# Half rotations of the tile two ahead put in front of the division of the probabilities on GpSimd

## The reference, cut to what matters

```python
for i in range(DEPTH):                                   # DEPTH = 6, 16 heads of 64, window 32
    x = attn_layer(shift_tokens(x), Wqkv[i], q_scale[i], k_scale[i], Wo[i]) + x
    x = ffn_layer(shift_tokens(x), ln_g[i], ln_b[i], W1[i], b1[i], W2[i], b2[i]) + x

def attn_layer(x, Wqkv, qs, ksc, Wo):
    q, k, v = split(x @ Wqkv)
    q = l2norm(q) * qs
    k = l2norm(k) * ksc
    q = q * cos * scale + rotate_half(q) * sin * scale
    k = k * cos * inv + rotate_half(k) * sin * inv
    sim = einsum(q, keys of this and the last window) * 8.0   # masked
    attn = softmax(sim)
    return (attn @ v) @ Wo
```

## Time and profile before

| | us |
|---|---|
| median of 3 runs | 2736.19 |
| the profiled execution | 2730.72 |
| its span | 2728.9 |
| VectorE busy | 1973.4 (72%) |
| TensorE busy, matmuls | 2169.6 (80%) |
| GpSimd busy | 1492.2 (55%) |
| ScalarE busy | 1509.5 (55%) |

### The profile page before, as it was taken

How to read it: one execution, slowest core, us unless ns; L and a number is a source line. 1 busy time by engine, 2 the same in 40 slices (tenths; PEclk the granted TensorE clock), 3 DMA queues, 4 the chain that set the end, 5 groups by cost and what they waited for, 6 DMA issues and landing times.

```text
span 2728.9 us, 53797 instructions
## 1 busy us (share of the span) xinstructions
PE 2169.6 (80%) x21684; PEld 1154.6 (42%) x21780; DVE 1973.4 (72%) x2087; ACT 1509.5 (55%) x1863; POOL 1492.2 (55%) x1031
## 2 busy tenths in 40 slices
PE   4768875888998989888889889889988756678734
PEld 1111123555555555555555555555555411111334
DVE  1766628888888888888888888888889426676211
ACT  2255564566676666666766676666766321455600
POOL 5500017777776776777776777777777234100033
PEclk7787897999999999999999999999999866897967
DMA  4100000000001000100010000000000001000133
GB/s 149 60 19 25 13 2 1 17 2 17 2 2 26 17 2 2 26 2 17 1 26 2 17 2 9 19 17 2 1 9 2 1 18 67 22 27 13 32 92 86
DMA packets 55828, 59.08 MB, mean 22 GB/s; under 512 B 13142, under 2 KB 45012, under 8 KB 55508
## 3 DMA queue, kind: packets, MB, share of 16 engines
q1 hardware_dynamic: 53444, 50.77, 6.1%
q0 software_dynamic: 2128, 4.72, 0.7%
HBM read 44.07 MB, written 11.01 MB: 20 GB/s over the span
## 4 chain that ended last, share of the span: by engine, by line
PE 36%; POOL 19%; DVE 17%; issue 16%; ACT 9%; DMA 2%; SPq 1%; POOLq 0%; DVEq 0%; ACTq 0%
PE bank L735 5%; PE bank L706 4%; PE bank L859 4%; DVE big L1463 4%; PE bank L923 4%; PE bank L933 4%; POOL big L580 3%; POOL big L597 3%; POOL big L581 3%; DVE big L1569 3%; POOL small L590 2%; ACT big L1180 2%; ACT pxs L1305 2%; PE bank L976 2%; DVE small L1563 2%
## 5 line engine op out<-in xcount | busy, mean ns | idle before, releaser
L1463 DVE TENSOR_REDUCE big<-bank 128x1 f32<-128x512 f32 x512 | 327.7, 685 | 199.3 <-PE bank L706 195.3
L602 POOL TENSOR_TENSOR sc<-sc,small 128x1024 f32<-128x1024 f32 x96 | 263.4, 2744 | 365.4 <-DVE small L1605 365.4
L859 PE MATMUL bank<-wqk,xs 128*128 128x512 f32 x768 | 359.2, 610 | 13.6 <-ACT xs L1261 8.3
L933 PE MATMUL bank<-pxs,mw 128*128 128x256 f32 x1536 | 366.2, 382 | 0.0
L1296 ACT ACTIVATE sc<-sc 128x1024 f32<-128x1024 f32 x96 | 101.5, 1057 | 464.0 <-DVE sc L1595 463.9
L933 PEld LDWEIGHTS bank<-pxs,mw 128*128 128x128 f32 x1536 | 291.1, 192 | 102.7 <-issue 71.9
L1180 ACT ACTIVATE big<-bank 128x1024 f32<-128x1024 f32 x256 | 250.2, 1026 | 140.1 <-PE bank L720 137.1
L1569 DVE TENSOR_TENSOR big<-big,rotCl 128x2048 f32<-128x2048 f32 x96 | 226.2, 2356 | 78.1 <-POOL big L581 78.1
L706 PE MATMUL bank<-pxs 48*128 48x512 bf16 x512 | 183.6, 439 | 117.1 <-DVE big L1463 74.0
L1563 DVE TENSOR_REDUCE small<-big 128x32 f32<-128x2048 f32 x96 | 219.0, 2281 | 39.5 <-ACT big L1274 30.2
L1584 DVE TENSOR_TENSOR big<-big,small 128x1024 f32<-128x1024 f32 x192 | 246.5, 1284 | 1.1 <-POOL small L592 1.1
(11 more groups left out here) (244 smaller groups left out, 3945.1 us busy)
## 6 DMA issues: line engine op xcount, KB each, us to landing
wqk<-in_L_ffn_Wqkv SPq DMA_DIRECT2D x12, 512.0 KB, 4.4
pxs<-part_rows SPq DMA_DIRECT2D x64, 96.0 KB
pxs<-part_rows SPq DMA_DIRECT2D x64, 64.0 KB
wqk<-in_L_ffn_w SPq DMA_DIRECT2D x16, 256.0 KB, 3.0
wvt<-in_wv_layers_t SPq DMA_DIRECT2D x6, 512.0 KB, 4.7
wol<-in_L_ffn_Wo SPq DMA_DIRECT2D x6, 512.0 KB, 5.8
part_rows<-big SPq DMA_DIRECT2D x24, 128.0 KB
part_rows<-sc SPq DMA_DIRECT2D x24, 128.0 KB
```

Of the source, the lines that this page charges most:

```text
L602: pool.tensor_tensor(p3, p3, rden(i).unsqueeze(2).broadcast_to([P, LH, 64]), ALU.mult).then_inc(l_pn, 1)
L859: m = pe.matmul(bank[:, 2 - 2 * half + c, :], xs[:, b % 2, WIN + i * P:WIN + (i + 1) * P], wqk[:, (2 * half + c) * 512:(2 * half + c + 1) ...
L933: m = pe.matmul(bank[:, 6, part * 2 * P:(part + 1) * 2 * P], mw[:, 2 * (a % 4) + s, a // 4, :], pxs[:, part, a, s, :], start=(a == 0 and s ...
L1463: dve.tensor_reduce(nm[:, qt, 2 * p + r:2 * p + r + 1], bank[:, 4 + r, :], AX.X, ALU.max, negate=True).then_inc(a_mx, 1)
```

## The change

On GpSimd, `normalise(T, i)` moves from in front of `turn_swapped(T + 2, ...)` to behind it, within the same slot. Nothing is added or removed.

```diff
@@ -611,12 +611,12 @@
                 if ahead >= 1:
                     inverse_root(T + 1, (i + 1) % 2)
                     add_keys(T + 1, (i + 1) % 2)
-                normalise(T, i)
                 if ahead >= 2:
                     if b == BATCH - 1 and i == 2:
                         pool.wait_ge(l_tab, 3 * l + 6)
                         settle(pool)
                     turn_swapped(T + 2, (i + 2) % TILES)
+                normalise(T, i)
```

## The result

The changed kernel takes 2763.96 us, the median of seven runs (2755.71 to 2768.84), against 2736.19 for the kernel before (seven runs). The ratio is 1.0103, 95% interval 1.0077 to 1.0129: 1% slower, 28 us. The prediction said 2772, and 2742 to 2825. The profiled execution took 2762.28 us with a span of 2760.5, 31.6 more than the one of before; the stretch from the first E to the last (E is the end of L1595) grew from 1715.4 to 1749.9 us, by 34.5, so that all of it lies in the layers.

A forecast was written before the change was run, and what follows sets the result against it. The prediction took a ring through reciprocals, division, half rotations and L1569 as the bound. Growth from E to L1569 of 37 us on the profiled 2730.72 gave 2768, and most of 5.5 on top 2772 us; range 2742 to 2825.

The forecast's parts named there:

- The ring: Loop closing a slot's time before the change: E, reciprocals, division, half rotations, L1569, next E; L1569 at E + 10.96.
- The sum from E to L1569: New path of evictions, half rotations with L1584's turn, division, transposition: 11.87 us, or 11.58 at i = 2.
- the turn of 1.08: The keys' L1584 on VectorE meets GpSimd's half rotations; they take turns, lengthening GpSimd's chain by 1.08 us.
- the 1.5 us given as a sign: Except at i = 2, VectorE's wait for the division would show mostly inside L1564, lasting 1.5 us or more.
- The transposition: L1612 on VectorE, directly ahead of L1569, waits for the division and joins the path: about 1.2 us more.
- Where the cost sits: Growth mainly in one slot of four, i = 2: E to L1569 11.58 against 10.27 us, +1.31.
- The sum was 37 us: Growth from E to L1569 over all slots: 6.2 us a layer, 37 us in six layers.
- The term that was put at nothing: From L1569 to the next E, VectorE's own operations, 6.24 us, taken as unchanged; ends -19 and +48 us.
- the 4 us that the forecast added for the median of before: Whole time: most of the 5.5 us by which the median before exceeds its profiled execution, put on top of 2768.
- L597 did wait for the end of L1569: Rival: at i = 2 GpSimd's key add L597 gets in before L1574, 53 us more, 2825 us; chance 0.08.
- The reciprocals did run beside L580: Rival: reciprocals L1605 take turns with GpSimd at i = 0 and 3, 24 to 53 us more; chance 0.07.
- The turn costs nothing: Rival: L1584 and the half rotations run side by side, E to L1569 10.9 us, 2685 us; chance 0.06.
- no change to be seen: Rival: shorter L1569, earlier L1584 for the queries and other engines take back two thirds, about 2748 us; chance 0.12.

The follow-up runs named there:

- keys_new: Changed kernel, with VectorE scaling the keys (L1584) directly behind the queries, ahead of sums and reciprocals: 2715.51 us, ratio 0.9954 to the kernel before.
- late_new: Changed kernel, with the transposition L1612 moved on VectorE from before L1569 to behind L1595: 2729.63 us, ratio 0.9989 to the kernel before.
- late_old: Kernel before, GpSimd's order kept, with the transposition L1612 moved on VectorE to behind L1595: 2767.3 us, ratio 1.0106 to the kernel before.
- i2_old: Changed kernel, but with the division first again in slots with i = 2 only: 2736.39 us, ratio 1.0011 to the kernel before.
- i2_new: Kernel before, with the half rotations ahead of the division in slots with i = 2 only: 2746.75 us, ratio 1.0068 to the kernel before.

## Why the prediction was right

*The ring.* That the reciprocals start the path before, and the evictions after, is in the waits (365.4 us to 16.2, and 340.2 on L1266). L580 starts at E + 3.00; the forecast had 3.06.

*The sum from E to L1569.* 11.87 was predicted for i = 0, 1 and 3, and 11.58 for i = 2. The means are 11.84 at i = 0, 11.79 at i = 1, 11.83 at i = 3 and 11.54 at i = 2. Its terms stand one by one in the slot shown: the turn of 1.08 (1225.18 to 1226.26), 2.2 for L581 after it (to 1228.49), 1.91 for the division. At i = 1 two terms were off against each other: L580 started at E + 3.20 and not 3.06, and the turn, inside its mean of 3.07 us, cost 0.7 and not 1.08. There L1564 was also shorter than the 1.5 us given as a sign, 1.12 in the mean, since VectorE reached it only at E + 9.39; it still stood until the division was through. The turn is shown by keys_new, where it goes and a microsecond with it. The transposition is shown by late_new and late_old in the sign, the same move gaining with one order and losing with the other, and in the size at i = 2 (-1.07 and +1.04 us). In the other kinds of slot the sizes are not equal and opposite: -1.34 and +0.48 at i = 3, -0.89 and +0.72 at i = 0, -0.01 and -0.40 at i = 1.

*Where the cost sits.* At i = 2, as said: i2_old takes away what is clear of noise, and i2_new alone brings back 14 to 19 of the 28 us. At i = 3 the table has +0.25 us a slot where the forecast has 0.26, but that agreement is in part luck. Batch by batch the trace has -0.65, +0.04, +0.88 and +0.61 (0 to 3), where the forecast had -0.72, +0.26, +0.91 and +0.59. The estimate for batch 1, a mean of the others, was 0.22 too high, and a layer's four such slots grew by 0.88 and not 1.04; in the mean over tiles 8 to 91 that doesn't show, because batch 2 counts six times in 21.

*What was off.* The sum was 37 us. In the means E to L1569 changed by -0.08, +0.07, +1.25 and +0.25 us at i = 0, 1, 2 and 3, where -0.13, +0.11, +1.31 and +0.26 stood; 24 x 1.49 is 36 us, and the layers grew by 34.5. The term that was put at nothing, L1569 to the next E, is -0.15, +0.06, -0.10 and +0.18: nothing in sum, though not in each. The two profiled executions differ by 31.6 and the medians by 28, so the 4 us that the forecast added for the median of before only took it further off.

*The rivals.* L597 did wait for the end of L1569, 12 times in the changed kernel (11 of them in the 24 slots with i = 2), and lost each time, for L1574's longest is 1306 ns. How it loses is in the rows of i2_new: at 1207.22 it comes 0.05 behind L1574 (L1577 there) and lasts 3.39 us. The reciprocals did run beside L580, at 1222.86, and took 0.25 us; 45 of the 96 lie wholly beside a GpSimd operation of over 1.5 us, and all 96 take 252 to 254 ns. That agrees with the list of the Trainium skill, "SBUF — State Buffer", section "Who interferes with whom". "The turn costs nothing" fell with the first slot. Of "no change to be seen" there was a part: i2_new shows that an earlier L1584 for the queries goes with 0.25 us less in the slot after, where that slot still divides first.

*What the forecast missed* is not in its number: the order is bad only beside VectorE's order. The growth came from two neighbours of the moved work, a scaling that met the half rotations and a transposition behind the division. With both moved on VectorE the same change on GpSimd gains 111 us.

## What to carry to other kernels

When a producer is taken off the head of a queue, look at what waits for the work that is now last, and at everything that stands behind that waiter on its engine; the gain is what was late before less what is late now, worked out per kind of slot. Operations of VectorE and GpSimd that hold each other up belong in each other's idle time, and a moved operation brings new pairs of them together. A reordering on one engine that loses may be the one that pays once the neighbour's queue is reordered with it, so test the two in all four combinations.

## What the runs showed of the hardware

- A reciprocal of 128x16 on VectorE isn't held up by a GpSimd operation beside it (0.25 us at 1222.86, L580 from 1222.82 on; 252 to 254 ns in all 96, 45 of them wholly beside one), while tensor_scalar is, at 128x32 (L1564, 1.90 instead of 0.18 us) and at 128x512 (L1644, 2.32 instead of 0.55).
- Where both engines waited for the end of the same VectorE instruction (L1569), VectorE's next one got in first in all 12 cases of the changed kernel: L1574 starts 0.03 or 0.04 us after that end, L597 0.08.
- An operation of VectorE with both operands in SBUF (L1584) and one of GpSimd (L580, L581) take turns, whole instructions at a time, also over a run of them: 3.23 us for L1584 and 3.35 for L581, 1.0 to 2.1 us of each spent standing.
